# Attention and FFN block on one Trainium2 core: the evacuation of a head's output, the next head's first PV block and one row-max step are put in another order

## The reference

```python
x  = L0_attn_x                       # (2, 2048, 256), fp32
xn = layernorm(x)
# attention: 16 heads of 16 columns, keys are the queries (k = q)
z  = layernorm(xn) * g + b
q  = z @ w_q.T + b_q ; v = z @ w_v.T + b_v
attn = softmax(q @ q.T / 4)          # per head and batch: 2048 x 2048
y1 = (attn @ v) @ w_out.T + b_out
# feed-forward with ternary weights
y2 = gelu(xn @ ternary(W1).T + b1) @ ternary(W2).T + b2
out = x + y1 + y2
```

## Time and profile before

| | before |
|---|---|
| median of 3 runs | 1406.68 us (1406.29 to 1407.9) |
| the profiled execution | 1406.08 us |
| its span, first to last instruction | 1404.4 us |
| TensorE busy | 1374.3 us (98%) |
| VectorE busy | 1330.8 us (95%) |
| ScalarE busy | 1240.6 us (88%) |
| GpSimd busy | 140.8 us (10%) |
| TensorE's granted clock | 0.995 of full speed, mean |
| DMA | 60.69 MB, 43 GB/s mean |

### The profile page before, as it was taken

One profiled execution on the slowest core, in us unless ns is written; L12 is line 12 of the kernel. 1 busy time (PEld: TensorE's weight loads), 2 busy tenths in 40 slices (PEclk: granted clock), 3 DMA queues, 4 the chain that ended last, 5 costly groups with the idle time before them and its releaser, 6 DMA issues.

```text
span 1404.4 us, 32258 instructions
## 1 busy us (share of the span) xinstructions
PE 1374.3 (98%) x13382; PEld 444.1 (32%) x13382; DVE 1330.8 (95%) x1397; ACT 1240.6 (88%) x2276; POOL 140.8 (10%) x350
## 2 busy tenths in 40 slices
PE   7999999999999999999999999999999999999998
PEld 5656643222222222222222222222222222222244
DVE  6898999999999999999999999999999999999934
ACT  5564638999999999999999999999999999999975
POOL 2101034000000000000000000000222200002100
PEclk8999999999999999999999999999999999999999
DMA  6011000000000000001000001011111110011121
GB/s 237 27 41 62 31 17 2 32 32 32 32 32 32 32 32 32 32 32 32 32 32 32 31 30 34 27 34 43 57 54 54 50 34 31 32 33 62 39 108 78
DMA packets 28796, 60.69 MB, mean 43 GB/s; under 512 B 6272, under 2 KB 11808, under 8 KB 28394
## 3 DMA queue, kind: packets, MB, share of 16 engines
q1 hardware_dynamic: 28074, 56.99, 11.9%
q10 hardware_dynamic: 576, 1.65, 0.3%
HBM read 41.29 MB, written 16.77 MB: 41 GB/s over the span
## 4 chain that ended last, share of the span: by engine, by line
PE 88%; DVE 7%; ACT 2%; issue 1%; DMA 1%; POOL 0%; ACTq 0%; DVEq 0%; POOLq 0%
PE ps L398 38%; PE ps L417 23%; PE ps L361 15%; DVE part_max L900 5%; PE ps L1214 3%; PE ps L1131 3%; PE ps L1151 2%; ACT w L1105 2%; PE ps L496 2%; PE ps L477 1%; DMA rows<-in_rows 1%; PE ps L466 1%; PE ps L506 0%; PE ps L1186 0%; DVE weight_scratch L892 0%
## 5 line engine op out<-in xcount | busy, mean ns | idle before, releaser
L900 DVE TENSOR_REDUCE part_max<-ps 128x1 f32<-128x1024 f32 x1024 | 1163.5, 1212 | 6.2 <-PE ps L361 3.7
L1105 ACT ACTIVATE w<-ps 128x512 f32<-128x512 f32 x2048 | 1111.3, 596 | 64.5 <-PE ps L417 22.9
L398 PE MATMUL ps<-w,v_ones 128*32 128x256 f32 (+1 forms) x7688 | 627.1, 398 | 0.6 <-DVE resid L821 0.3
L417 PE MATMUL ps<-qry,key 50*128 50x512 f16 x1984 | 410.5, 386 | 8.2 <-ACT w L1105 7.1
L361 PE MATMUL ps<-qry,key 48*128 48x512 f16 x2048 | 404.2, 379 | 4.8 <-DVE part_max L900 4.7
L398 PEld LDWEIGHTS ps<-w,v_ones 128*32 128x32 f32 x7688 | 152.2, 107 | 382.0 <-issue 210.4
L417 PEld LDWEIGHTS ps<-qry,key 50*128 50x128 f16 x1984 | 100.7, 92 | 440.7 <-ACT w L1105 413.9
L361 PEld LDWEIGHTS ps<-qry,key 48*128 48x128 f16 x2048 | 101.7, 95 | 29.7 <-issue 11.1
L692 POOL COPY v_ones<-v_all 128x128 f32<-128x128 f32 x64 | 18.6, 291 | 760.6 <-PE ps L398 760.6
L1067 ACT ACTIVATE q_split<-q_by_factor,sigma_bq 128x512 f16<-128x512 f32 x16 | 11.1, 719 | 63.4 <-DVE q_by_factor L802 62.9
L1214 PE MATMUL ps<-x,w_ternary 128*128 128x512 f16 x256 | 62.0, 381 | 1.6 <-ACT hidden L1071 1.6
(11 more groups left out here) (154 smaller groups left out, 506.7 us busy)
## 6 DMA issues: line engine op xcount, KB each, us to landing
key<-q_parts SPq DMA_DIRECT2D x62, 128.0 KB
qry<-q_parts SPq DMA_DIRECT2D x62, 128.0 KB
o_heads<-o_evacuated SPq DMA_DIRECT2D x31, 256.0 KB, 9.8
key<-q_parts SPq DMA_DIRECT2D x66, 64.0 KB
qry<-q_parts SPq DMA_DIRECT2D x66, 64.0 KB
resid<-in_x SPq DMA_DIRECT2D x8, 512.0 KB, 13.5
q_parts<-q_split SPq DMA_DIRECT2D x16, 256.0 KB, 2.3
out<-resid SPq DMA_DIRECT2D x7, 512.0 KB, 3.2
```

The costliest lines, as they stand in the source:

```text
L398: mm = eng.matmul(pv[32 * c:32 * c + 2 * D, c0:c1], vst[:, kb, :], prob[kb % 2][:, c * BANK + c0:c * BANK + c1], start=(kb == 0), stop=(kb ...
L417: eng.matmul(ring_bank(v, i, False), key[v][r:r + KROWS, kb * P:(kb + 1) * P], qry[v][r:r + KROWS, c * BANK:(c + 1) * BANK], start=True, s ...
L900: dve.tensor_reduce(part_max[h % 2][:, blk, side:side + 1], pa[a % 2], AX.X, ALU.max).then_inc(s_r, 1)
L1105: act.activation(prob[kb % 2][:, c * BANK:(c + 1) * BANK], ring_bank(k, i, last), ACT.Exp, scale=exp_scale).then_inc(s_e, 1)
```

## The change

`EVAC_AT` goes from 4 to 3: ScalarE copies the output of the last head behind the fourth exponential of a head instead of behind the fifth. In the first period of every head but head 0 (and the last head, which doesn't run through `pe_head`) TensorE takes a new order. The fourth group, B6 B7 A P, becomes B6 P B7 A: block 0's PV product stands between the two score products, and the row-max step behind both. The next group's B8 and B9 then follow that row-max step directly. Nothing is added or left out, and no tile or semaphore is new. The last head takes the new `EVAC_AT` alone.

```diff
 PERIOD = "BBAPBBAPBBAPBBAP"
+PERIOD_EVAC = "BBAPBBAPBBAPBPBA"
...
-        EVAC_AT = 4
+        EVAC_AT = 3
...
-                for what in PERIOD:
+                for what in PERIOD_EVAC if q == 0 and not first else PERIOD:
```

## The result

The changed kernel takes 1420.03 us (median of 6 runs, 1419.03 to 1421.32), the kernel before 1406.66 (6 runs, 1406.29 to 1407.9). The ratio is **1.0094, 95% interval 1.0084 to 1.0105**: 13.4 us slower, where 12.7 were forecast.

A forecast was written before the change was run, and what follows sets the result against it. The chain is TensorE's, but VectorE is slower within a head, so its lateness is paid almost in full. 29 x 0.46 = 13.3, reciprocals + 0.2, head 30 + 0.35, last head - 1.1: +12.7 us, 1419.4 us; range 1415.8 to 1422.2.

The forecast's parts named there:

- Steps 1 to 3 and 5: Head's start: block 0 at 615.72, B7 at 616.72, row-max pair 11 0.96 late; on VectorE reduction 12 0.51 late.
- The small waits: TensorE, within a head: waits for VectorE of 0.02 us a step, from about row-max step 16 on.
- Step 6: Row-max step 35: its pair, with 0.06 us to spare, starts 0.46 us later, not recovered at the next head's start.
- Step 4: TensorE after row-max step 11: PV block 1 waits for exponential 7, making its list 0.01 to 0.02 us a head longer.
- head 30 and the way to the last head: Head 30 feeds only row-max steps to 31, where the slack is 0.15 us: + 0.35 us.
- the reciprocals: Two heads with a reciprocal in VectorE's list: the 0.11 us slack each had left is already spent, + 0.2 us.
- The range: Whole kernel: 1415.8 to 1422.2 us, from 0.35 to 0.55 us a head and 0 to -1.3 us in the last head.
- the rival "faster": Head's start: VectorE loses nothing, TensorE gains its stall back; 6.2 us less, 1400.5 us; chance 0.07.
- The rule of the Trainium skill: Rank engines by occupancy, TensorE not by matmul time, and seek gaps on the highest; TensorE's 0.24 us isn't worth mending.

The follow-up runs named there:

- the last experiment: Kernel before, with block 0 naming its evacuation wait first and, in the last head alone, the evacuation behind the fourth exponential: 1403.56 us, ratio 0.9988.

## Why the prediction was right

**The mechanism holds by its own steps.** Steps 1 to 3 and 5 came out within 0.02: block 0 is 0.57 behind B6 (0.58 said), B7 at 1.57 (1.58), reduction 12 late by 0.51 (0.51). The small waits before L362 are there, 21.4 us of idle on VectorE was 20 in the forecast, and VectorE kept its 1.131. The run with the row-max step last and the short reductions show that VectorE's lateness, not B7's, is the price in the changed kernel.

**Step 6 was short by 0.03, and had the tightest step wrong.** It said 0.46 a head, with 0.06 to spare at step 35; measured is 0.49, with the last wait at step 32. What was missing is the second wait on that step. In the kernel before, reduction 30 and the pair of step 32 read:

```profile
638.36 1.21 DVE L900 TENSOR_REDUCE part_max<-ps 128x1 f32<-128x1024 f32 x1
...
639.74 0.38 PE L361 MATMUL ps<-qry,key 48*128 48x512 f16 x2
```

The pair stands 0.17 behind the reduction's end, and it needs 0.14 to 0.15, so only some 0.03 was to spare there: 0.51 - 0.03 is the measured price within 0.01. Behind step 32 TensorE loses nothing more, as step 35 shows. With the second wait moved away step 35 is the tightest, and a head costs 0.44, where the forecast's own terms gave 0.46.

**Step 4 was wrong in sign.** I had TensorE's own list 0.01 to 0.02 a head longer, because PV block 1 would wait 0.15 behind exponential 7. The 0.15 was block 0's, with its several waits; a block with one late wait takes 0.05. From B6 to PV block 1 it was 623.25 - 620.60 = 2.65 after, and 617.88 - 615.14 = 2.74 in the earlier trace rows (2.73 by the unrounded starts): 0.08 shorter. Nothing of it showed, since VectorE set the time; that this error did the sum no harm was luck. It also moved the small waits: they begin at step 13, not 16.

**The sum in measured terms:** 29 heads x 0.49 = 14.2; head 30 and the way to the last head + 0.33 (0.35 said); the last head - 1.25 (- 1.1 said, since no exponential held the next B back); the reciprocals about + 0.1 (0.2 said). That is 13.4, the difference of the medians. That the forecast of the whole came out 0.6 us low hides two misses that partly cancel: 0.9 too little for the 29 heads, some 0.3 too much in the other terms.

**The range.** Its upper end doesn't follow from its own terms: 29 x 0.55 + 0.2 + 0.35 with nothing from the last head is 16.5 us, which gives 1423.2 and not 1422.2. The measured 1420.03 lies inside either.

**Two readings that I announced failed.** VectorE's share of the chain did not rise above half; it stayed at 7%. And the rival "faster" lost not because TensorE gains nothing: its list is 0.08 shorter up to PV block 1, and with the short reduction at step 12 a head is 0.03 shorter.

The rule of the Trainium skill that stood beside the sum ("Perfetto Trace Analysis", Identifying the Most-Contended Engine) agrees with the runs in one part: the gap that opened on VectorE, the engine with the most busy time within a head, cost 0.49 us a head. (The looking for gaps stands in that page's next section, Optimization Strategy.) The other part of what was drawn from it, that TensorE's stall isn't worth mending, the runs don't bear out. In the last experiment block 0 came 0.045 us earlier, VectorE's list was as before, and the head was 0.045 shorter. Before the change TensorE's list set the time, although VectorE had slightly more busy time. What bounds a changed head is a ring of both: 20 reductions at VectorE's pace (11 to 30), then TensorE's own list from step 32 to the next head's step 11.

## What to carry to other kernels

Before moving an instruction ahead of others, look at the engine that consumes what they make. Here the consumer's pace was slower than the producer's (1.131 against 1.109 us a step), and the time that it was late at one point came back in full, although two pairs of banks lie between, less only the slack at the tightest later point. Find that point by following the gap between the two engines over a whole period, not around the edit, and count at each step how many waits the instruction has. A step can also come too early: then the producer waits, and what stands behind it on its list is late. And where an instruction has several waits, name the one that is met last first.

## What the runs showed of the hardware

**Several waits on one instruction.** A TensorE instruction with one late wait starts its product 0.05 us after the producer's end; with the late wait named second or third, 0.14 to 0.15. In both places the trace has a separate semaphore instruction ahead of the weight load. The weight load itself carries the wait that the program names first, and the semaphore instruction those named after it: at block 0 of the changed kernel it ends at 621.12, and the product starts at 621.17. In the run with the late waits first the semaphore instruction ends at 618.77, long before the evacuation does (619.17), and the weight load waits for the evacuation itself. Three runs moved or reordered such waits and took 0.05 to 0.14 a head off.

**TensorE's clock and the scatter of runs.** In the profiled execution of the changed kernel TensorE waits 1.39 us for VectorE behind the first reciprocal, and then the granted clock is at 1.2 GHz for 3.4 us; the windows show it (columns in the row):

```profile
core 0: us, PE busy (x) PEld busy (x) DVE busy (x) ACT busy (x) POOL busy (x), PEclk, DMA share, GB/s
905.00:909.00 4.00, 2.61 (x30) 0.78 (x32) 4.00 (x4) 2.38 (x5) 1.02 (x5) 1.00 0.00 0
909.00:912.40 3.40, 3.40 (x25) 0.74 (x25) 3.04 (x3) 2.23 (x5) 0.00 (x0) 0.50 0.01 3
```

That head is 1.0 us longer than the other terms explain, which is about the 1.1 us by which this execution lies above its median; no trace of the other five executions can confirm it. The same stretch stayed at 2.4 GHz in the kernel before, with a wait of 1.37, and it fell again in the run with the moved wait but in none of the nine other experiments. The length of the wait alone doesn't decide it: it was 1.46 us both in the run with the moved wait, where the clock fell, and in the one with the late waits first, where it didn't. What decides isn't settled. Near the end of the feed-forward stage the same happens in some executions. The windows of the run with the last head's edit, and of the one with the short reduction at step 12:

```profile
203.00:211.00 8.00, 7.37 (x33) 3.06 (x33) 5.87 (x6) 1.55 (x2) 8.00 (x13) 0.57 0.02 4
```

```profile
203.00:211.00 8.00, 7.70 (x57) 3.97 (x57) 8.00 (x9) 2.27 (x4) 8.00 (x13) 1.00 0.02 4
```

The first has 6.8 us at the lower clock in that stage, and its first evacuation starts at 253.6 us; the kernel before, with the same order up to there, has 3.4 us and starts it at 251.9. The second has none there and starts it at 249.8; the changed kernel has 3.4 us and starts it at 251.8. Single runs that differ by 1 or 2 us therefore say little here; the head's length, which repeats within 0.01 us in all but a few heads of a run, says more.
